# AdaLN transformer layer on one core: both score layouts as two 64-row tiles on TensorE, causal mask by matmuls, row maxima by whole-bank reductions

## The chip, the cores and the metric

The kernel runs on one core of a Trainium2 chip. The metric is the device time of one execution in microseconds (us); the median of three runs of the kernel before is 1957.38 us (1954.21 to 1957.84). TensorE (PE) multiplies, VectorE (DVE), ScalarE (ACT) and GpSimd (POOL) do the rest, SyncE (SP) issues all DMA transfers. PE writes to PSUM (eight banks of 128 partitions x 512 fp32), from which DVE and ACT read.

## The reference, cut to what matters

A layer over x of shape (32, 512, 256), with 16 heads of 16 dimensions:

```python
h = _layernorm(x) * (1 + ca) + sa
q, k, v = split(h @ w_qkv.T + b_qkv)                     # 16 heads of 16
scores = einsum('bhqd,bhkd->bhqk', q, k) / np.sqrt(hd)
scores = scores + where(k_pos <= q_pos, -(q_pos - k_pos), -1e30)   # ALiBi and causal mask
out = einsum('bhqk,bhkd->bhqd', softmax(scores), v)
x = x + ga * (out @ w_out.T + b_out)
h = _layernorm(x) * (1 + cb) + sb
x = x + gb * ffn(h)                                      # gate of 8 experts, top-p count, two experts used
```

The modulation vectors (sa, ca, ga, sb, cb, gb) come from a small product before the layer.

## The kernel before, in words

**Stages.** Each of the 32 batch elements passes through stages of a software pipeline: layer norm and transposition, q/k/v, row maxima, scores and exponentials, weighting of v, output product, second norm, gate, experts. One iteration of the main loop (`iterations`, `one`) has 16 slots, one head of scores in each. The tables `SIDE`, `SP_AT`, `DVE_AT`, `POOL_AT` and `ACT_AT` say which other step ("side step") of which batch element stands in which slot; `PE_ORDER`, `ACT_ORDER` and `DVE_ORDER` are the order within a slot. Every engine executes its own list in order, and semaphores tie the lists together. No planner moves anything.

**Two layouts of the scores.** The exponentials need the scores with keys on partitions ("scores", `0 1 2` in the order strings, banks 0 to 2 of PSUM, L575). Their row maximum is needed first, and is taken from a second computation with queries on partitions ("row scores", `a b c`, banks 3 and 4 in turn, L589), which runs eight heads ahead. Only the ten causal 128x128 blocks of a head's sixteen are computed: 1280 moving columns in each layout. Both contract over one stack of rows: 96 rows hold q and k split into high and low fp16 parts for a pair of heads (the rows of the other head are zeros in `kz`), then the ALiBi row and mask rows up to 112, then the negated maxima up to 114. So each matmul uses all 128 rows of the array, for a head of 16 dimensions.

**Maxima.** DVE reads the pieces a (512 columns), b (384 and 128) and c (256) with `tensor_tensor_reduce`, which adds the mask of the diagonal block (`mask_qk`) and reduces to one column of `mxt` (L853). Each of the four instructions of a head is followed by an instruction that fetches the accumulator. A group of four heads is transposed by PE (side step `mt`, L538), copied by ACT to `negm` and put by DMA into the stack (`load_aug`). PE may write piece k only when DVE has read piece k-2 (`mx_read`).

**Exponentials and weighting.** ACT takes exp of banks 0 to 2 (L647). POOL zeroes the upper triangles of the diagonal blocks by `affine_select` (L1018, semaphore `masked`). PE multiplies with v (`weigh`, L603 and L609), fp32, four heads side by side in 32 output columns each; `w` stands in every slot with one key tile kt, and is a burst of 4 x 128 columns, with a second of 4 x 384, 256 or 128 where kt is 0, 1 or 2.

**Side steps.** qk, v, out and moe are groups of fp16 matmuls of 3072 columns (L497); they use banks 6 and 7 in turn, and each waits for the reader of the step before it in its bank. DVE reads the result of a side step one slot later (`S`, `U`).

## Time and profile before

| | us |
|---|---|
| median of 3 runs | 1957.38 |
| profiled execution, span from first to last instruction | 1953.2 |
| PE busy | 1724.6 (88%) |
| PE weight loads busy | 995.6 (51%) |
| DVE busy | 1552.6 (79%) |
| ACT busy | 1214.8 (62%) |
| POOL busy | 998.9 (51%) |

The page of the profile gives no time outside the span; the lowest run is 1954.21 us, 1.0 us more than the span. Busy time is the union of the instructions' durations. A matmul's duration contains the way of its results through the array, which the next matmul overlaps, so the pitch (start to start) of neighbouring rows tells more of PE than its busy time. The granted TensorE clock, in forty slices of the span, is 8 and 7 tenths in the first two, 9 tenths or more in the next 36, and 8 and 6 tenths in the last two.

### The profile page before, as it was taken

To read this page: it belongs to the slowest core of one execution; us is meant where nothing else is said; L and a number is where in the kernel's file an instruction comes from. 1 tells how busy PE (TensorE), PEld (TensorE's weight loads), DVE (VectorE), ACT (ScalarE), POOL (GpSimd) and SP (SyncE) were. 2 spreads that over 40 slices of the span, in tenths; PEclk is the share of its full clock that TensorE was granted. 3 is DMA by queue.
4 is the path that set the end of the run, shared out by engine and by line. 5 is a ranking of instruction groups with operands and counts; after the bars stand their busy time and mean duration, and the time that the engine had idled before them with its cause. 6 is when DMAs were issued, how large, how long until landed. Compare 5 with 4: busy or idle time off the path is not lost.

```text
span 1953.2 us, 62334 instructions
## 1 busy us (share of the span) xinstructions
PE 1724.6 (88%) x17744; PEld 995.6 (51%) x17744; DVE 1552.6 (79%) x5632; ACT 1214.8 (62%) x2466; POOL 998.9 (51%) x1225
## 2 busy tenths in 40 slices
...
GB/s 131 77 133 116 125 119 128 141 128 124 125 104 125 140 136 126 120 125 120 128 141 128 123 125 104 126 141 136 125 120 125 121 129 139 131 123 115 120 88 45
DMA packets 206753, 238.21 MB, mean 122 GB/s; under 512 B 27626, under 2 KB 153138, under 8 KB 206674
## 3 DMA queue, kind: packets, MB, share of 16 engines
...
q8 instruction: 23, 0.38, 0.1%
...
## 4 chain that ended last, share of the span: by engine, by line
PE 49%; DVE 24%; issue 18%; ACT 4%; DMA 2%; DVEq 2%; POOL 1%; SPq 1%; ACTq 0%; POOLq 0%
PE ps L497 18%; PE ps L589 12%; DVE ps L853 9%; PE ps L575 8%; PE ps L609 4%; PE ps L603 4%; DVE mxt L853 4%; DVE ol L868 2%; DVEq L257 1%; ACT hf_a L658 1%; ACT hh_a L660 1%; DVE qk_st L793 1%; DVE st_c L759 1%; ACT prob L647 1%; PE ps L515 1%
## 5 line engine op out<-in xcount | busy, mean ns | idle before, releaser
L853 DVE CUSTOM_DVE_ANT_0 ps<-ps,mask_qk 128x512 f32<-128x512 f32 (+3 forms) x2048 | 971.1, 510 | 296.3 <-PE ps L589 285.3
L647 ACT ACTIVATE prob<-ps 128x512 f32<-128x512 f32 (+1 forms) x1536 | 743.5, 530 | 363.2 <-PE ps L575 362.3
L589 PE MATMUL ps<-kz,qs 112*128 112x512 f16 (+3 forms) x2048 | 542.4, 307 | 138.2 <-DVE mxt L853 129.5
L1018 POOL TENSOR_SCALAR_AFFINE_SELECT prob<-prob 128x512 f32<-128x512 f32 x512 | 353.4, 696 | 364.2 <-ACT prob L647 364.2
L575 PE MATMUL ps<-qs,kz 114*128 114x128 f16 (+2 forms) x3584 | 453.3, 243 | 3.7 <-DMA qs<-negm 3.1
L589 PEld LDWEIGHTS ps<-kz,qs 112*128 112x128 f16 x2048 | 187.1, 97 | 492.8 <-DVE mxt L853 308.6
L853 DVE DVE_READ_ACCUMULATOR2_ANT mxt<- 128x1 f32 x2048 | 288.6, 141 | 0.0
L575 PEld LDWEIGHTS ps<-qs,kz 114*128 114x128 f16 x3584 | 259.7, 98 | 50.5 <-ACT prob L647 3.8
L609 PE MATMUL ps<-prob,va 128*32 128x384 f32 (+2 forms) x3072 | 237.0, 380 | 0.0
L603 PE MATMUL ps<-prob,va 128*32 128x128 f32 x4096 | 218.3, 285 | 2.0 <-issue 0.9
L679 ACT ACTIVATE qk_st<-ps,bqk 128x512 f16<-128x512 f32 x128 | 88.0, 688 | 97.7 <-PE ps L497 95.7
L992 POOL TENSOR_TENSOR xg<-xc,ga_bc 128x1024 f32<-128x1024 f32 x32 | 75.6, 2361 | 101.6 <-DMA ga_bc<-rows_d 90.5
L986 POOL TENSOR_TENSOR om<-oc,rz 128x1024 f32<-128x1024 f32 x32 | 75.5, 2359 | 95.3 <-DMA rz<-rz_d 95.3
L603 PEld LDWEIGHTS ps<-prob,va 128*32 128x32 f32 x4096 | 81.1, 108 | 84.6 <-issue 81.7
L965 POOL TENSOR_TENSOR rs_c<-ve_c,neg_half 128x4 f32<-128x4 f32 x32 | 32.7, 1022 | 166.4 <-DVE nm_c L774 166.4
L793 DVE SCALAR_TENSOR_TENSOR qk_st<-ps,bqk,qk_st 128x512 f16<-128x512 f32 x128 | 95.6, 747 | 7.1 <-ACT qk_st L679 7.1
L497 PE MATMUL ps<-moe_hi,hh_c 128*128 128x512 f16 x256 | 99.5, 389 | 1.0 <-DVE gsub L826 1.0
L1008 POOL TENSOR_TENSOR zg<-zs,gb_bc 128x512 f32<-128x512 f32 x64 | 81.4, 1271 | 36.1 <-DVE zs L806 35.1
L695 ACT ACTIVATE z<-ps,scl 128x256 f32<-128x256 f32 x128 | 60.5, 473 | 62.9 <-PE ps L497 58.8
L497 PE MATMUL ps<-moe_lo,hh_c 128*128 128x512 f16 x256 | 99.2, 387 | 0.0
L497 PE MATMUL ps<-moe_hi,hl_c 128*128 128x512 f16 x256 | 99.1, 387 | 0.0
L497 PE MATMUL ps<-hh_a,wqkv_hi 128*128 128x512 f16 x256 | 97.9, 382 | 0.4 <-DVE qk_st L793 0.4
...
## 6 DMA issues: line engine op xcount, KB each, us to landing
qk_d<-qk_st SPq DMA_DIRECT2D x128, 256.0 KB, 2.0
ou_d<-ou SPq DMA_DIRECT2D x128, 256.0 KB, 2.0
qs<-qk_d SPq DMA_DIRECT2D x128, 192.0 KB, 2.6
kz<-qk_d SPq DMA_DIRECT2D x256, 96.0 KB, 2.6
...
qk_d<-qk_st SPq DMA_DIRECT2D x128, 128.0 KB, 1.9
...
```

Of the source, the lines that this page charges most:

```text
L497: x_ = mm(dst, a, b, start=(n == 0), stop=(n == len(pairs) - 1))
L575: x_ = mm(ps[:, ST + n, col:col + w * P], kz[0:STACK, h, kt * P:(kt + 1) * P], qs[0:STACK, h // 2, qt * P:(qt + w) * P], start=True, stop= ...
L589: x_ = mm(ps[:, bank, col:col + w], qs[0:CONST, h // 2, qt * P:(qt + 1) * P], kz[0:CONST, h, 0:w], start=True, stop=True)
L603: x_ = mm(ps[32 * j:32 * j + 32, PVB, kt * P:(kt + 1) * P], va[:, kt, h, :], prob[:, h % 8, kt * P:(kt + 1) * P], start=(kt == 0), stop=(k ...
L609: x_ = mm(ps[32 * j:32 * j + 32, PVB, (kt + 1) * P:S], va[:, kt, h, :], prob[:, h % 8, PCOL[kt]:PCOL[kt] + w], start=False, stop=False)
L647: nc.scalar.activation(prob[:, h % 8, at:at + w], ps[:, ST + n, 0:w], ACT.Exp, scale=1.0 / FS).then_inc(s["exp_done"], 1)
L679: nc.scalar.activation(qk_st[:, k, 0, :], src, ACT.Identity, bias=bqk[:, 2 * k + n // 2:2 * k + n // 2 + 1]).then_inc(s["qk_hi"], 1)
L793: v.scalar_tensor_tensor(qk_st[:, kk, 1, :], src, bqk[:, 2 * kk + n // 2:2 * kk + n // 2 + 1], qk_st[:, kk, 0, :], ALU.add, ALU.subtract). ...
L853: x_ = v.tensor_tensor_reduce(ps[:, bank, col:col + w], ps[:, bank, col:col + w], mask_qk[:, S - w:S], 1.0, -3e38, ALU.add, ALU.max, mxt[: ...
L992: q.tensor_tensor(xg[:], xc[:], ga_bc[:, 1:2, :].broadcast_to([P, QT, D]), ALU.add).then_inc(s["xg_ready"], 1)
L1008: q.tensor_tensor(zg[:, t, :], zs[:, t, :], gb_bc[:].rearrange("p (o d) -> p o d", o=1).broadcast_to([P, 2, D]), ALU.mult).then_inc(s["zg_ ...
L1018: q.affine_select(out=d, in_=d, compare_op=ALU.is_ge, fill=0.0, base=0, pattern=[[0, 4], [1, P]], channel_multiplier=-1).then_inc(s["maske ...
```

## The change: what it does

- **Stack.** A head now has its own 64 rows (`HALF`): even heads in partitions 0 to 63, odd heads in 64 to 127: 48 rows of q and k parts, the ALiBi row (49 in all for the row scores) and the maxima row (50 for the scores). `kz` is stored per pair of heads, no zeros are needed, and the mask rows are gone.
- **PE.** `both` issues a matmul of the scores of head t and one of the row scores of head `pos ^ 1` alternately. The two are always in opposite halves of the array's rows and in different banks. The waits for `exp_done` and `mx_read` stand together ahead of the piece.
- **Mask.** In piece 0 of each layout two matmuls (64 rows of a bf16 table of 0 and -1e30 against a repeated identity, 256 columns each) are put into the bank first, and the products of the four diagonal blocks are added. `mask` on POOL and the semaphore `masked` go.
- **Maxima.** Pieces are 4, 4 and 2 blocks. One `tensor_reduce` per piece writes one maximum per block into `mxp`; once per four heads a further `tensor_reduce` (`r`, `rows_max`) gives `mxt`, with absent blocks preset to -3e38. `mt` is one transpose instead of four and ACT copies 16x128 instead of 4x512.
- **Order.** Even slots: `01su2`, odd: `0su12w`; `w` stands only in odd slots with two key tiles (0 and 3, or 1 and 2). Two `v` steps, the `spread` steps and some banks of `SIDE` move.
- **DMA.** A stack load is four transfers of 48 partitions instead of three, `load_aug` is two transfers as before, with 256-byte pieces.

```diff
-PE_ORDER = "01asub2wc"
-ACT_ORDER = "o01su2"
-DVE_ORDER = "SUaboc"
+PE_ORDER = ("01su2", "0su12w")
+ACT_ORDER = ("o01su2", "o0su12")
+DVE_ORDER = "rSUaboc"
 SIDE = {
...
-    5: [("mt", 2, 0, 1)],
-    6: [("gate", 0, -2, 0)],
-    7: [("qk", 2, 1, 1), ("v", 0, 1, 0)],
+    5: [("mt", 2, 0, 1), ("v", 0, 1, 0)],
+    6: [("gate", 0, -2, 1)],
+    7: [("qk", 2, 1, 0)],
...
-    13: [("mt", 0, 1, 0)],
+    13: [("mt", 0, 1, 1), ("v", 1, 1, 0)],
     14: [("out", 0, -1, 1)],
-    15: [("v", 1, 1, 1), ("out", 1, -1, 0)],
+    15: [("out", 1, -1, 0)],
...
+        BLOCKS = [4, 4, 2]
+        MX_AT = [(0, 5), (11, 1), (7, 1)]
+        MOVES = [6, 2, 2]
+        ROWS_AT = [[(0, 0, 1, 0), (1, 1, 1, 1), (2, 2, 1, 2), (3, 3, 1, 3)], [(3, 0, 3, 1), (2, 1, 1, 0)],
+                   [(1, 0, 1, 0), (2, 0, 1, 1)]]
...
+            def score(b, h, n, m):
+                rows = slice(HALF * (h % 2), HALF * (h % 2) + ST_ROWS)
+                half = slice(HALF * (h % 2), HALF * (h % 2) + HALF)
+                bank = ps[:, ST + n, :]
+                if n == 0 and m < 2:
+                    x_ = mm(bank.rearrange("p (t k) -> p t k", t=QT)[:, :, HALF * m:HALF * m + HALF], mask_key(2 + m)[half],
+                            EYE[half].rearrange("p (t k) -> p t k", t=QT), start=(m == 0), stop=False)
+                else:
+                    kt, qt, w = CHUNK[n][m - 2 if n == 0 else m]
+                    col = sum(c[2] for c in CHUNK[n][:m - 2 if n == 0 else m]) * P
+                    x_ = mm(bank[:, col:col + w * P], kz[rows, h // 2, kt * P:(kt + 1) * P],
+                            qs[rows, h // 2, qt * P:(qt + w) * P], start=(n > 0), stop=(n > 0 or m == 5))
...
+            def both(i, t, n):
+                bm, pos = max_at(i, t)
+                hm = pos ^ 1
+                if live(i):
...
+                    wait(pe, "exp_done", i * 48 + 3 * t + n - 2, "passed_pe")
+                if live(bm):
...
+                    wait(pe, "mx_read", bm * 48 + 3 * pos + n - 1, "passed_pe")
+                for m in range(MOVES[n]):
+                    if live(i) and not (n == 2 and m == 1):
+                        score(i, t, n, m)
+                    if live(bm):
+                        row_score(bm, pos, hm, n, m)
...
+            def maxima(b, pos, n):
+                g, h = pos // 4, pos ^ 1
+                at = (h % 2) * 2 + h % 4 // 2
+                wait(dve, "mx_ready", b * 48 + 3 * pos + n + 1, "passed_dve")
+                bank = ps[:, MX + (3 * pos + n) % 2, 0:BLOCKS[n] * P]
+                first, apart = MX_AT[n]
+                v.tensor_reduce(mxp[:, g % 2, at, first:first + apart * (BLOCKS[n] - 1) + 1:apart],
+                                bank.rearrange("p (m k) -> p m k", k=P), AX.X, ALU.max).then_inc(s["mx_read"], 1)
```

On PE, before, the end of one slot of the loop and the start of the next read as follows (L575 scores, L589 row scores, L603 and L609 weighting with v):

```order
L589 MATMUL ps<-kz,qs 128x384 [waits mx_read]
L589 MATMUL ps<-kz,qs 128x128
L575 MATMUL ps<-qs,kz 128x256 [waits exp_done]
L603 MATMUL ps<-prob,va 32x128 x4
L609 MATMUL ps<-prob,va 32x256 x4
L257 REGISTER_ALU
L589 MATMUL ps<-kz,qs 128x256 [waits mx_read]
L575 MATMUL ps<-qs,kz 128x128 [waits exp_done]
L575 MATMUL ps<-qs,kz 128x128 x3
```

Now the end of an odd slot and the start of the even one after it (L586 and L602 mask matmuls, L591 scores, L606 row scores, L637 and L643 weighting):

```order
L259 REGISTER_ALU [waits exp_done]
L591 MATMUL ps<-qs,kz 128x256 [waits mx_read]
L606 MATMUL ps<-kz,qs 128x128 x2
L637 MATMUL ps<-prob,va 32x128 [waits ou_ready,va_ready,exp_done]
L637 MATMUL ps<-prob,va 32x128 x3
L643 MATMUL ps<-prob,va 32x384 x4
L637 MATMUL ps<-prob,va 32x128 x4
L259 REGISTER_ALU [waits exp_done]
L586 MATMUL ps<-mk 128x4x64 [waits mx_read]
L602 MATMUL ps<-mk 128x4x64
L586 MATMUL ps<-mk 128x4x64
L602 MATMUL ps<-mk 128x4x64
```

The two layouts alternate row by row now, the weighting follows both, and a piece of scores waits for DVE too.

On DVE, before, around the step o_lo (L868) of slot 11 (L853 maxima, L806 the side step moe):

```order
L853 ISA ps,mxt<-ps,mask_qk 128x512 [waits mx_ready]
L853 ISA mxt 128x1
L257 REGISTER_ALU
L853 ISA ps,mxt<-ps,mask_qk 128x384 [waits mx_ready]
L853 ISA mxt 128x1
L853 ISA ps,mxt<-ps,mask_qk 128x128
L853 ISA mxt 128x1
L257 REGISTER_ALU [waits om_ready]
L868 SCALAR_TENSOR_TENSOR ol<-om,bv,oh 128x512 [waits out_ready,oh_ready]
L868 SCALAR_TENSOR_TENSOR ol<-om,bv,oh 128x512
```

Now the maxima of two slots, with the group's further reduction between them (L882 maxima, L888 rows_max, L825 the side step qk):

```order
L882 TENSOR_REDUCE mxp<-ps 128x4 [waits mx_ready]
L259 REGISTER_ALU
L882 TENSOR_REDUCE mxp<-ps 128x2 [waits mx_ready]
L888 TENSOR_REDUCE mxt<-mxp 128x16 [waits mx_read,mt_ready]
L259 REGISTER_ALU
L825 SCALAR_TENSOR_TENSOR qk_st<-ps,bqk,qk_st 128x512 [waits qk_hi]
```

Eight instructions per head became three, and one more per four heads.

## Rows read from the trace of the kernel before

**Rows 1.** The page: busy time by engine, and shares of the chain of waits.
```profile
PE 1724.6 (88%) x17744; PEld 995.6 (51%) x17744; DVE 1552.6 (79%) x5632; ACT 1214.8 (62%) x2466; POOL 998.9 (51%) x1225
PE 49%; DVE 24%; issue 18%; ACT 4%; DMA 2%; DVEq 2%; POOL 1%; SPq 1%; ACTq 0%; POOLq 0%
```
**Rows 2.** Windows: length, busy PE, PEld, DVE, ACT, POOL, then clock, DMA share, GB/s.
```profile
1000.00:1057.70 57.70, 52.52 (x553) 30.36 (x553) 47.75 (x176) 37.86 (x77) 30.88 (x38) 1.00 0.38 126
```
**Rows 3.** Timeline, PE, the gate: start us, duration us, engine, line, operation.
```profile
1000.95 0.17 PE L497 MATMUL ps<-gw_hi,hh_c 128*128 128x8 f16 x1
...
1001.53 0.17 PE L497 MATMUL ps<-gw_hi,hl_c 128*128 128x8 f16 x1
...
1578.23 0.17 PE L497 MATMUL ps<-gw_hi,hh_c 128*128 128x8 f16 x1
```
**Rows 4.** Timeline, PE, one slot and its borders.
```profile
1010.40 0.43 PE L603 MATMUL ps<-prob,va 128*32 128x128 f32 x8
1010.65 0.83 PE L609 MATMUL ps<-prob,va 128*32 128x384 f32 x8
1011.41 0.28 PE L589 MATMUL ps<-kz,qs 112*128 112x256 f16 x1
1011.53 0.61 PE L575 MATMUL ps<-qs,kz 114*128 114x128 f16 x6
1011.97 0.38 PE L589 MATMUL ps<-kz,qs 112*128 112x512 f16 x1
1012.19 0.60 PE L538 MATMUL ps<-ident,mxt 128*4 128x128 f32 x4
1012.77 0.39 PE L497 MATMUL ps<-hh_a,wqkv_hi 128*128 128x512 f16 x1
...
1014.07 0.38 PE L589 MATMUL ps<-kz,qs 112*128 112x384 f16 x2
...
1014.50 0.43 PE L603 MATMUL ps<-prob,va 128*32 128x128 f32 x8
1014.74 0.61 PE L609 MATMUL ps<-prob,va 128*32 128x256 f32 x8
1015.29 0.28 PE L589 MATMUL ps<-kz,qs 112*128 112x256 f16 x1
```
**Rows 5.** Timeline, DVE: the gate chain's ends, one head's maxima, ot, o_lo.
```profile
1004.17 0.18 DVE L824 TENSOR_REDUCE gmax<-ps 128x4 f32<-128x32 f32 x1
...
1006.88 0.70 DVE L853 CUSTOM_DVE_ANT_0 ps<-ps,mask_qk 128x512 f32<-128x512 f32 x1
1007.49 0.14 DVE L853 DVE_READ_ACCUMULATOR2_ANT mxt<- 128x1 f32 x1
...
1008.64 0.75 DVE L793 SCALAR_TENSOR_TENSOR qk_st<-ps,bqk,qk_st 128x512 f16<-128x512 f32 x1
...
1021.76 2.89 DVE L868 SCALAR_TENSOR_TENSOR ol<-om,bv,oh 128x512 f16<-128x512 f32 x2
```
**Rows 6.** Timeline, ACT, the slot with the side steps ta.
```profile
1038.48 1.08 ACT L647 ACTIVATE prob<-ps 128x512 f32<-128x512 f32 x2
1039.66 0.78 ACT L658 ACTIVATE hf_a<-ps,mod_a 128x512 f32<-128x512 f32 x1
...
1042.32 1.37 ACT L647 ACTIVATE prob<-ps 128x256 f32<-128x256 f32 x3
```
**Rows 7.** Waits: engine, line, releaser: us in total, times, longest.
```profile
DVE ps L853 <- PE ps L589: 285.3, 416, 3.9
PE ps L589 <- DVE mxt L853: 129.5, 200, 4.1
```
**Rows 8.** One line's instructions: min/median/max ns, first and last start.
```profile
L1018 POOL TENSOR_SCALAR_AFFINE_SELECT prob<-prob x512: 624/635/1104, 75.0 to 1891.4; 128x512 f32<-128x512 f32 x171
L868 DVE SCALAR_TENSOR_TENSOR ol<-om,bv,oh x64: 739/1114/1865, 158.1 to 1918.1; 128x512 f16<-128x512 f32 x64
```
**Rows 9.** The page: the costliest groups, the weight loads of the scores.
```profile
L575 PEld LDWEIGHTS ps<-qs,kz 114*128 114x128 f16 x3584 | 259.7, 98 | 50.5 <-ACT prob L647 3.8
```

More of the change, by code:

```diff
@@ L535, in side_step @@
                 elif name == "mt":
-                    wait(pe, "mx_read", b * 48 + 12 * (n + 1))
-                    for t in range(QT):
-                        x_ = nc.tensor.transpose(dst[0:4, t * P:(t + 1) * P], mxt[:, n, t, :], ident[:])
-                    x_.then_inc(s["mt_ready"], 1)
+                    wait(pe, "mxt_ready", b * 4 + n + 1)
+                    nc.tensor.transpose(dst[0:16, 0:P], mxt[:, n, :], ident[:]).then_inc(s["mt_ready"], 1)
                 elif name == "out":
@@ L566, in side_step @@
                     products(dst, pairs).then_inc(s["moe_ready"], 1)
-            def scores(b, h, n):
-                if h % 4 == 0 and n == 0:
-                    wait(pe, "aug_loaded", (b * 4 + h // 4 + 1) * 32)
-                wait(pe, "exp_done", b * 48 + 3 * h + n - 2)
-                col = 0
-                for kt, qt, w in CHUNK[n]:
-                    x_ = mm(ps[:, ST + n, col:col + w * P], kz[0:STACK, h, kt * P:(kt + 1) * P],
-                            qs[0:STACK, h // 2, qt * P:(qt + w) * P], start=True, stop=True)
-                    col += w * P
-                x_.then_inc(s["st_ready"], 1)
@@ new lines, in row_score @@
+            def row_score(b, pos, h, n, m):
+                rows = slice(HALF * (h % 2), HALF * (h % 2) + MX_ROWS)
+                half = slice(HALF * (h % 2), HALF * (h % 2) + HALF)
+                bank = ps[:, MX + (3 * pos + n) % 2, :]
+                if n == 0 and m < 2:
+                    x_ = mm(bank.rearrange("p (t k) -> p t k", t=QT)[:, :, HALF * m:HALF * m + HALF], mask_key(m)[half],
+                            EYE[half].rearrange("p (t k) -> p t k", t=QT), start=(m == 0), stop=False)
+                else:
+                    qt, kt, w, col = ROWS_AT[n][m - 2 if n == 0 else m]
+                    x_ = mm(bank[:, col * P:(col + w) * P], qs[rows, h // 2, qt * P:(qt + 1) * P],
+                            kz[rows, h // 2, kt * P:(kt + w) * P], start=(n > 0), stop=(n > 0 or m == 5))
+                if m == MOVES[n] - 1:
+                    x_.then_inc(s["mx_ready"], 1)
@@ L618, in one @@
                         experts()
-                    bm, hm = max_at(i, t)
                     bp = i if t >= 4 else i - 1
-                    for what in PE_ORDER:
-                        if what in "012" and live(i):
-                            scores(i, t, int(what))
-                        if what in "abc" and live(bm):
-                            row_scores(bm, hm, "abc".index(what))
+                    for what in PE_ORDER[t % 2]:
+                        if what in "012":
+                            both(i, t, int(what))
                         if what in "su":
@@ L688, in side_step @@
                     wait(act, "aug_loaded", (b * 4 + n) * 32)
-                    nc.scalar.activation(negm[:], ps[0:4, MISC + bank, :], ACT.Copy,
+                    nc.scalar.activation(negm[:], ps[0:16, MISC + bank, 0:P], ACT.Copy,
                                          scale=-1.0 / FS).then_inc(s["nm_ready"], 1)
@@ L725, in one @@
                         act.wait_ge(s["ld_w"], W_LOADS * 16)
-                    for what in ACT_ORDER:
+                    for what in ACT_ORDER[t % 2]:
                         if what in "012" and live(i):
```

162 lines of the change are left out of this document (74 added, 88 removed).

## Prediction

> **What bounds the kernel now.** I read the busy times and the chain of waits first. PE is busy 88% of the span and holds 49% of the chain, DVE 79% and 24%, and 18% of the chain is issue, that is the gaps of hand-overs [rows 1]. So PE and DVE bound it by turns. The waits agree: DVE waits 285.3 us for row scores, PE 129.5 us for the maxima [rows 7], each for the other.
>
> Then the period. The gate's first matmul stands at 1000.95 and ten iterations later at 1578.23 [rows 3]: 57.7 us each. In one such period PE is busy 52.52 us, DVE 47.75, ACT 37.86, POOL 30.88, at the full clock of 2.4 GHz [rows 2]. The diagonal masks run from 75.0 to 1891.4 us, 16 per iteration [rows 8]; I take 31 full periods (the last is thinner), and the 165 us of start and end as unchanged.
>
> Last, one slot on PE where nothing waits [rows 4]. From 1011.41 to 1015.29 it takes 3.88 us: mt 0.58 (1012.19 to 1012.77), qk 1.30 (to 1014.07), weighting 0.79 (1014.50 to 1015.29), the rest 1.21. The eleven score matmuls stream 2560 columns; the six at 1011.53 stream 1024 in 0.44 us, 2.33 a ns, so all of them take 1.10. The wide part of the weighting takes 0.76 with 384 columns (from 1010.65) and 0.55 with 256 (from 1014.74): 0.21 per 128, so 384 columns stream in 0.64 and 0.12 are left for the change from 32-column tiles back to the whole array. Two such changes of shape make 0.24 a slot.
>
> **The cost per pair of slots, before.** The orders alternate after the change, so I add up pairs (slots 0 and 1, 2 and 3, ...). PE: score work and shape changes 2.7 a pair; qk, v, moe, out 1.3 each; ta or t2 0.9 (two times mt's 0.44); gate 0.6 [rows 3]; mt 0.58; weighting of key tiles 0 to 3: 0.85, 0.64, 0.43, 0.21. That gives 5.7, 6.0, 5.7, 6.6, 7.4, 6.0, 6.1, 7.3: 50.7 us, against 52.52 busy, which holds the matmuls' tails. DVE: maxima 1.76 a slot (1006.88 to 1008.64); qk 0.66 and other 512-column steps 0.61 (1006.88 to 1007.49), the moe half 0.4 (half as wide), gates 2.7 (1004.17 to 1006.88), o_lo 2.8, reciprocal, statistics and their ends 0.7 to 0.9 each [rows 5]: 7.5, 4.2, 5.4, 7.1, 4.6, 7.4, 6.4, 4.1: 46.6. ACT: exponentials 1.3 a slot, ta or t2 2.66, a bank's copy 0.5 [rows 6]: 6.2 in the pairs with ta and t2, less elsewhere. The larger of the three in each pair: 7.5, 6.0, 6.2, 7.1, 7.4, 7.4, 6.4, 7.3, in all 55.2. The period is 57.7, so 2.5 us are hand-overs which this sum doesn't see. I keep them.
>
> **The change part by part.**
> Scores on PE. Per slot 1280 columns in either layout, plus 2 x 256 for each layout's mask: 1792 in each half of the array. Side by side they take 1792/2.33 = 0.77 us instead of 1.10; one after the other 1.54. The trace shows no row tiles. The nearest row is the weighting: eight matmuls of 384 columns in four column tiles take 0.64 and the shape change [rows 4]. In turn, at 2.33 columns a ns, eight would take 1.32. So tiles of the array do run at once, and I take 0.78. It saves 0.32 x 16 = 5.1 us a period; at the other end it costs 7.0. The mask matmuls write their 256 columns as four pieces of 64; if that halved their rate, 0.22 a slot would come back, 3.5 us a period; the rows show no such output, and I take 0.
>
> The Trainium skill, page "TensorE: Matmul & The Clock Gate", Part 3, says that four row tiles measured 3.07x, which is in line with the value taken; no run here shows it yet.
>
> Shape changes. `w` in every second slot drops some, but scores and full-array side steps now have different shapes: two in an even slot (01|su|2), four in an odd one (0|su|12|w|). 48 a period instead of 32 and the mt steps' own. A row split may need no such gap, or the same 0.12: 0 to 48 x 0.12 = 5.8 against 4.0 before. I take 0.12: +1.8 us.
>
> The Trainium skill, "TensorEngine Tiling (Array Packing)", Tiling Modes, Key Properties, says that a change of mode drains the engine while a change of tile does not. The gap of 0.12 agrees for column tiles [rows 4]; were it free between the whole array and row tiles, 32 of the 48 changes would go, 3.8 us a period on PE.
>
> mt: 3 of 4 transposes go, 0.33 x 4 = 1.3 us. PE per pair after: 3.35 (scores 1.56, six changes 0.72, weighting 1.07) and the side steps: 4.5, 6.0, 5.8, 5.3, 6.2, 6.0, 6.2, 6.0, in all 46.0.
>
> Maxima on DVE. Two pieces of 512 and one of 256 stay reads of PSUM at one element a cycle: 1280 elements before and after. `tensor_reduce` of 512 is not in the trace. Below: 0.55 (512 at the slope between 128x32 at 0.18 and the 512 of L853). Above: 0.75 as L793 [rows 5]. I take the pitch of 0.61 of the instruction it replaces, 0.35 for 256: 1.57 a slot, 0.19 less; what goes is the fixed part of two pieces, the accumulator reads being hidden already (the one at 1007.49 starts with the next piece). `rows_max` adds 0.2 per four slots, +0.8. Bounds: 1.4 to 1.9 a slot, -5.8 to +2.2 us a period; taken -2.2. DVE per pair after: 7.3, 3.8, 5.2, 6.7, 4.4, 7.0, 6.3, 3.8: 44.5.
>
> POOL loses 512 masks of 0.64 us [rows 8], on no bound now. What it may give is o_lo, whose halves take 739 to 1865 ns with POOL busy beside them: 0 to 1.4 us a period; I take nothing, since zg and res of `finish` still stand there. `mask` also stood ahead of `weigh`; PE hardly waited at it, so 0.
>
> ACT: negm of 128 columns instead of 512, 4 x 0.3 = 1.2 us, partly exposed in the two ACT pairs, but one `v` copy joins the t2 pair: 5.9 and 6.4.
>
> The joint wait. Ahead of each piece PE now waits for exp and for DVE together, and what stands behind is the scores for ACT too. Where DVE is in gates or o_lo (2.7, 2.8 us), PE stops after two more pieces, as before. Bound: 0 (it would have stopped there anyway) to 0.2 a slot, 3 us; I take 0. One more DMA per stack load lies eight heads ahead of its use: 0; without that cover it would cost an issue, some 0.5 us.
>
> **Sum.** Larger of three per pair: 7.3, 6.0, 6.4, 6.7, 6.2, 7.0, 6.3, 6.0 = 51.9; with the 2.5 us of hand-overs 54.4. Five of the eight pairs are DVE's or ACT's now, which is why 4.7 us off PE give only 3.3 a period. 3.3 x 31 = 102 us off the span of 1953.2: 1851, and with the 4.2 us by which the median stands above the span, 1855. Own range 1810 to 1905.
>
> **The rivals.**
> 1. *The tiles don't overlap* (slower). If the two halves run in turn, score work is 1.54 a slot: PE per pair +1.5: 6.0, 7.5, 7.3, 6.8, 7.7, 7.5, 7.7, 7.5. With DVE's 7.3 in the first pair 59.3 + 2.5 = 61.8 us, +4.1 x 31: 2085. It decides from 1.1 us a slot upward. For it: each layout now writes a whole bank's 128 partitions, twice the results at once, which column tiles never did. Against it: the overlap in rows 4, and that this split leaves weights and moving rows in separate partitions. 11%.
> 2. *Weight loads bound the score work.* 19 loads instead of 11 per slot, most of them under 128-column matmuls. If each took its recorded 98 ns [rows 9] in turn, a slot's scores would take 1.86 us, PE per pair +2.2: with DVE's 7.3 in the first pair 63.8 + 2.5 = 66.3, +8.6 x 31: 2225. Against it: the gate's 24 matmuls with 128x128 weights stand 25 ns apart (1000.95 to 1001.53) [rows 3], and the six at 1011.53 take no more than their columns [rows 4], so the recorded 98 ns overlap. 3%.
>
> The Trainium skill, "TensorE: Matmul & The Clock Gate", Back-to-back issue gap, gives about 81 ns for a matmul of 128 columns with its load; by that, 19 of them would take an estimated 1.54 us, as in rival 1. The gate rows don't bear it out.
>
> 3. *Single slots bind, not pairs.* The work is uneven now: an even slot has 1.0 and its side step on PE, an odd one 2.3 and its side steps. With two banks for maxima and three for scores there is little to run ahead. The larger engine slot by slot sums to 56.4 after and 58.7 before (measured: 57.7), a gain of 2.3 x 31 = 71: 1886. With the joint wait at its 3 us a period it is slower by 0.7 x 31 = 22: 1979. Middle: 1925. For it: the issue share of 18% [rows 1], which says how much the engines hand to and fro. Against: an odd slot puts its two DVE pieces ahead of `w`, whose 1.07 covers DVE. 20%.
> 4. *The order hides the DVE stretches.* If `su` covers the maxima throughout, groups of four slots decide: 11.1 (DVE), 11.9 (DVE), 12.2, 12.2 = 47.4, with hand-overs 49.9, with o_lo shorter 49.1: 1690 to 1715. For it: the way back to PE is shorter by the accumulator read of 0.14. Against: five of eight pairs are not PE's. 12%.
>
> **Numbers.** Forecast 54%, rival 3 20%, rival 4 12%, rival 1 11%, rival 2 3%. Likeliest 1855. Range 1710 to 1960: it leaves out half of rival 4 and rivals 1 and 2, 20%, and of rival 3 only its last part. About 0.2%, 4 us, is what can be told from no change. Rival 3 gives 16% to faster, 2% to no change and 2% to slower; so faster 82%, same 2%, slower 16%.
>
> **What would show it.** Right: row scores and scores of a pair start within a few ns of each other, a slot's score rows span 0.78 us of pitch, `tensor_reduce` of 512 has a pitch of 0.61, the gate repeats every 54.4 us, DVE waits less for PE than 285 us, POOL near 650 us busy. Each change of shape around `su` shows 0.12. Wrong: pairs in turn (1.54), a mask matmul longer than its 256 columns (its output lies in four pieces of 64), PE idle behind `mx_read` by over 3 us a period more than now (rival 3), or a period under 51 (rival 4).

## The result, and the profile after

The changed kernel takes 2065.76 us (median of 4 runs, 2060.84 to 2069.36) against 1957.61 us before: 1.055 times as long, 95% interval 1.0536 to 1.0572. It is slower by 108 us where 1855 us had been forecast. The profiled execution took 2060.84 us, its span is 2059.1.

The page after, busy times and chain of waits, answers to [rows 1]:

```profile
PE 1646.7 (80%) x21456; PEld 963.5 (47%) x21456; DVE 1430.0 (69%) x3200; ACT 1187.9 (58%) x2466; POOL 647.9 (31%) x711
PE 40%; issue 16%; DVE 14%; DMA 11%; POOL 7%; ACT 6%; SPq 4%; DVEq 1%; ACTq 1%; POOLq 1%
```

No engine is busier than before, yet the span is longer. PE and DVE together held 73% of the chain and hold 54% now; DMA, POOL and SP's queue rose from 4% to 22%. So a larger part of the chain now runs through short transfers and what waits for them, where [rows 1] showed 4%.

One window of an iteration's length after, the gate's first matmul of two successive iterations, and the clock around one stretch (columns as in [rows 2, 3]):

```profile
1000.00:1061.20 61.20, 50.18 (x672) 29.22 (x668) 44.15 (x99) 36.93 (x78) 20.37 (x23) 0.94 0.36 119
...
1032.00:1033.00 1.00, 0.27 (x1) 0.09 (x1) 0.86 (x3) 1.00 (x2) 0.02 (x1) 1.00 0.34 73
1033.00:1034.00 1.00, 0.40 (x4) 0.14 (x4) 1.00 (x3) 1.00 (x4) 0.00 (x0) 1.00 0.15 41
1034.00:1035.00 1.00, 0.00 (x0) 0.00 (x0) 1.00 (x3) 0.65 (x3) 0.00 (x0) 0.75 0.00 0
1035.00:1036.00 1.00, 0.83 (x15) 0.63 (x19) 1.00 (x4) 0.38 (x1) 0.00 (x0) 0.50 0.01 2
1036.00:1037.00 1.00, 1.00 (x12) 0.33 (x8) 0.81 (x7) 0.00 (x0) 0.00 (x0) 0.50 0.01 2
```
```profile
992.55 0.18 PE L511 MATMUL ps<-gw_hi,hh_c 128*128 128x8 f16 x1
...
1053.78 0.18 PE L511 MATMUL ps<-gw_hi,hh_c 128*128 128x8 f16 x1
```

An iteration takes 61.2 us (mean of 20: 61.25), 57.7 before and 54.4 in the forecast. The granted clock is 0.94 where it was 1.00: after 0.27, 0.40 and 0.00 us of work in three successive microseconds PE falls to 1.2 GHz and stays there for 6.8 us. From 200 to 1850 us this happens 28 times, 170.7 us in all; in the same part of the kernel before it happens not once (there are such stretches only at its start and end). The Trainium skill, "TensorE: Matmul & The Clock Gate", Part 1, section "A second HAM failure mode: psum-queue depth-cycling", describes a kernel whose short idle spells between groups of matmuls made the clock swing between its two levels; the rows above agree.

What such a stretch costs can be read in the changed kernel itself, because its length varies. Two successive iterations, the first with 6.8 us at 1.2 GHz and the second with 3.4:

```profile
262.10:323.50 61.40, 50.07 (x673) 29.24 (x669) 44.18 (x99) 36.96 (x78) 20.07 (x22) 0.94 0.37 119
323.50:383.09 59.59, 48.65 (x673) 28.68 (x669) 44.18 (x99) 36.96 (x78) 20.06 (x22) 0.97 0.38 122
```

The same instructions take 1.8 us less. PE's busy time alone differs by 1.4 us; the rest is a shorter wait ahead of slot 12.

The timeline of PE after, scores (L586, L591) and row scores (L602, L606), answers to [rows 4]:

```profile
1005.64 0.40 PE L637 MATMUL ps<-prob,va 128*32 128x128 f32 x8
1005.98 0.28 PE L586 MATMUL ps<-mk 64*128 64x256 bf16 x1
1005.98 0.28 PE L602 MATMUL ps<-mk 64*128 64x256 bf16 x1
1006.10 0.27 PE L586 MATMUL ps<-mk 64*128 64x256 bf16 x1
...
1006.21 0.22 PE L591 MATMUL ps<-qs,kz 50*128 50x128 f16 x1
...
1006.43 0.32 PE L591 MATMUL ps<-qs,kz 50*128 50x384 f16 x1
1006.43 0.32 PE L606 MATMUL ps<-kz,qs 49*128 49x384 f16 x1
1006.60 0.22 PE L591 MATMUL ps<-qs,kz 50*128 50x128 f16 x1
1006.60 0.22 PE L606 MATMUL ps<-kz,qs 49*128 49x128 f16 x1
1006.75 0.39 PE L511 MATMUL ps<-moe_hi,hh_c 128*128 128x512 f16 x1
...
1008.15 0.28 PE L591 MATMUL ps<-qs,kz 50*128 50x256 f16 x1
...
1008.27 0.27 PE L602 MATMUL ps<-mk 64*128 64x256 bf16 x1
```

The two tiles do run at once: both of a pair start within 0.02 us of each other. A slot's scores take 0.45 (1005.98 to 1006.43), 0.22 (two pitches up to the change of shape) and 0.12 us (1008.15 to 1008.27): 0.79, forecast 0.78. The mask matmul's four pieces of 64 cost nothing (256 columns in 0.11 or 0.12). A change of shape is 0.10: the last pair, 0.05 long, starts at 1006.60 and the experts' matmul at 1006.75.

Four pairs of 128 columns pass in 0.22 us, though a weight load still records 97 ns, as in [rows 9] (the page after):

```profile
L591 PEld LDWEIGHTS ps<-qs,kz 50*128 50x128 f16 x3584 | 271.3, 97 | 389.6 <-issue 337.9
```

DVE after, by form (count, busy us, mean ns, idle before it), and the o_lo step (min/median/max ns), answering to [rows 5, 8]:

```profile
L882 DVE TENSOR_REDUCE mxp<-ps 128x4 f32<-128x512 f32 x1024 | 674.7, 686 | 279.8 <-PE ps L606 279.7
L882 DVE TENSOR_REDUCE mxp<-ps 128x2 f32<-128x256 f32 x512 | 212.7, 415 | 111.5 <-PE ps L606 109.8
```
```profile
L901 DVE SCALAR_TENSOR_TENSOR ol<-om,bv,oh x64: 736/792/1875, 162.6 to 2024.8; 128x512 f16<-128x512 f32 x64
```

Two of them in a row take 1.29 us (0.69 + 0.60), so the pitch of 512 is 0.60, forecast 0.61. The o_lo step fell from a median of 1114 to 792 ns, 0.6 us an iteration: a gain that the forecast had left at zero.

The waits after, answering to [rows 7]; the last two rows are one transfer chain, after and before:

```profile
DVE mxp L882 <- PE ps L606: 389.6, 485, 2.8
PE ps L591 <- DVE mxp L882: 170.7, 137, 2.2
POOL om L1023 <- DMA rz<-rz_d: 197.8, 32, 8.5
POOL om L986 <- DMA rz<-rz_d: 95.3, 31, 3.6
```

Both engines wait longer for each other, PE in fewer waits that are longer on average (1.25 us for 0.65). In an iteration PE stands still for 10.9 us in gaps of over 0.15 us; before, it was 5.1. The largest gaps, as means, stand in slot 1 (0.49 ahead of mt, 1.03 and 1.41 ahead of pieces 1 and 2), slot 5 (1.00 ahead of v), slot 7 (1.60 ahead of piece 2, DVE in the gate chain), slot 12 (1.15 and 1.38 ahead of pieces 0 and 1) and slot 13 (1.11 ahead of v). In the two of slot 12 PE waits for ACT, which comes late to the exponentials because it first rounds POOL's product, and then for DVE, which is in o_lo. Both hang on these rows (SP, POOL, DVE):

```profile
1000.26 0.52 SPq L414 DMA_DIRECT2D rz_d<-zr  x1
1002.28 1.28 SPq L420 DMA_DIRECT2D rz<-rz_d  x2
...
1008.02 2.35 POOL L1023 TENSOR_TENSOR om<-oc,rz 128x1024 f32<-128x1024 f32 x1 [6.02 <-DMA rz<-rz_d]
...
1011.91 2.52 DVE L901 SCALAR_TENSOR_TENSOR ol<-om,bv,oh 128x512 f16<-128x512 f32 x2 [0.42 <-ACT oh L746]
```

The reciprocals are stored and loaded back behind four stack transfers in slot 8. Store, load, POOL's product and ACT's rounding take 11.6 us from issue to o_lo. Before, DVE waited for this input of o_lo twice in the whole kernel, 5.0 us in all; now it waits 32 times, 27.6 us. (In the kernel before PE also stood still 1.5 us behind o_lo, so only a part of the two gaps is new.)

### The profile page after: what moved, and what is told of

Read it like the earlier page. It is cut to its first block, busy times and chain, and to the rows that moved or that the text cites. A ratio compares the mean times of both kernels' runs of the same rounds, so it can differ in the third digit from the quotient of the medians.

```text
span 2059.1 us, 69066 instructions
## 1 busy us (share of the span) xinstructions
PE 1646.7 (80%) x21456; PEld 963.5 (47%) x21456; DVE 1430.0 (69%) x3200; ACT 1187.9 (58%) x2466; POOL 647.9 (31%) x711
## 4 chain that ended last, share of the span: by engine, by line
PE 40%; issue 16%; DVE 14%; DMA 11%; POOL 7%; ACT 6%; SPq 4%; DVEq 1%; ACTq 1%; POOLq 1%
PE ps L511 16%; DMA rz<-rz_d 7%; DVE mxp L882 7%; PE ps L591 7%; PE ps L643 6%; PE ps L637 5%; POOL om L1023 4%; DMA rz_d<-zr 3%; PE ps L586 3%; ACT hh_c L692 2%; POOL x L1037 2%; PE ps L606 2%; DVE ol L901 1%; SPq L385 1%; ACT oh L746 1%
## 5 line engine op out<-in xcount | busy, mean ns | idle before, releaser
L882 DVE TENSOR_REDUCE mxp<-ps 128x4 f32<-128x512 f32 (+1 forms) x1536 | 874.6, 596 | 391.2 <-PE ps L606 389.6
L591 PE MATMUL ps<-qs,kz 50*128 50x128 f16 (+2 forms) x3584 | 494.2, 247 | 183.4 <-DVE mxp L882 170.7
L606 PE MATMUL ps<-kz,qs 49*128 49x128 f16 (+1 forms) x4096 | 502.5, 239 | 2.7 <-DVE mxp L882 2.7
L591 PEld LDWEIGHTS ps<-qs,kz 50*128 50x128 f16 x3584 | 271.3, 97 | 389.6 <-issue 337.9
L606 PEld LDWEIGHTS ps<-kz,qs 49*128 49x128 f16 x4096 | 286.9, 97 | 10.5 <-DVE mxp L882 5.2
L586 PE MATMUL ps<-mk 64*128 64x256 bf16 x1024 | 203.8, 280 | 76.5 <-ACT prob L679 33.8
L643 PE MATMUL ps<-prob,va 128*32 128x384 f32 (+2 forms) x3072 | 257.5, 408 | 0.0
L637 PE MATMUL ps<-prob,va 128*32 128x128 f32 x4096 | 226.9, 296 | 1.0 <-ACT ou L734 0.8
L602 PE MATMUL ps<-mk 64*128 64x256 bf16 x1024 | 207.6, 284 | 5.1 <-DVE mxp L882 2.6
L637 PEld LDWEIGHTS ps<-prob,va 128*32 128x32 f32 x4096 | 113.1, 115 | 116.5 <-issue 72.2
L586 PEld LDWEIGHTS ps<-mk 64*128 64x128 bf16 x1024 | 66.2, 95 | 154.7 <-issue 146.6
L511 PE MATMUL ps<-hh_a,wqkv_hi 128*128 128x512 f16 x256 | 111.4, 435 | 12.3 <-DVE zs L838 11.6
L511 PE MATMUL ps<-wqkv_hi,hh_a 128*128 128x256 f16 x256 | 71.8, 280 | 60.4 <-DVE zs L838 30.0
L734 ACT ACTIVATE ou<-ps 128x512 f32<-128x512 f32 x128 | 76.8, 600 | 63.2 <-PE ps L643 63.1
L511 PE MATMUL ps<-hl_a,wqkv_hi 128*128 128x512 f16 x256 | 108.6, 424 | 0.0
L511 PE MATMUL ps<-hh_a,wqkv_lo 128*128 128x512 f16 x256 | 104.7, 409 | 0.0
L825 DVE SCALAR_TENSOR_TENSOR qk_st<-ps,bqk,qk_st 128x512 f16<-128x512 f32 x128 | 95.3, 744 | 9.4 <-ACT qk_st L711 9.0
## 6 DMA issues: line engine op xcount, KB each, us to landing
qk_d<-qk_st SPq DMA_DIRECT2D x128, 256.0 KB, 2.0
ou_d<-ou SPq DMA_DIRECT2D x128, 256.0 KB, 2.0
oc<-ou_d SPq DMA_DIRECT2D x64, 256.0 KB
```

The costliest lines, as they stand in the source:

```text
L511: x_ = mm(dst, a, b, start=(n == 0), stop=(n == len(pairs) - 1))
L586: x_ = mm(bank.rearrange("p (t k) -> p t k", t=QT)[:, :, HALF * m:HALF * m + HALF], mask_key(2 + m)[half], EYE[half].rearrange("p (t k) -> ...
L591: x_ = mm(bank[:, col:col + w * P], kz[rows, h // 2, kt * P:(kt + 1) * P], qs[rows, h // 2, qt * P:(qt + w) * P], start=(n > 0), stop=(n > ...
L602: x_ = mm(bank.rearrange("p (t k) -> p t k", t=QT)[:, :, HALF * m:HALF * m + HALF], mask_key(m)[half], EYE[half].rearrange("p (t k) -> p t ...
L606: x_ = mm(bank[:, col * P:(col + w) * P], qs[rows, h // 2, qt * P:(qt + 1) * P], kz[rows, h // 2, kt * P:(kt + w) * P], start=(n > 0), sto ...
L637: x_ = mm(ps[32 * j:32 * j + 32, PVB, kt * P:(kt + 1) * P], va[:, kt, h, :], prob[:, h % 8, kt * P:(kt + 1) * P], start=(kt == 0), stop=False)
```

## The experiments

Unless said otherwise, an edit is made on the changed kernel. Times are medians of 4 runs (10 for e16), ratios are to the kernel before with their 95% intervals; before had 1957.2 to 1957.9 us beside them. "Half clock" is the number of stretches at 1.2 GHz from 200 to 1850 us and their total.

**e4: do the tiles overlap?** Row scores take the head of the same half of the array.

```diff
-                hm = pos ^ 1
+                hm = pos
-                g, h = pos // 4, pos ^ 1
+                g, h = pos // 4, pos
```

> The changed kernel with the row scores taken from a head of the same parity as the scores beside them, so that both matmuls of a pair use the same 64 rows of the array and can't run at once. It says what the overlap is worth. If PE's streaming still sets much of the period: 0.7 us a slot more on PE, less what lies in gaps: 5 to 10 us a period, 2220 to 2370. If the overlap is mostly spent in gaps by now (waits and the clock set the period): under 3 us a period, 2066 to 2160; PE would then also be busier and the clock higher than 0.93.

2298.71 us, 1.1715 [1.1674, 1.1757], 233 us above the changed kernel (half clock 20 times, 207.6 us). The same pair now runs in turn (timeline of PE in e4):

```profile
1006.75 0.33 PE L591 MATMUL ps<-qs,kz 50*128 50x384 f16 x1
1006.93 0.33 PE L606 MATMUL ps<-kz,qs 49*128 49x384 f16 x1
```

0.18 apart instead of 0.00. The overlap is real and worth 233 us; it isn't what went wrong. The Trainium skill, "TensorE: Matmul & The Clock Gate", Part 3, measures 3.07 times the speed for four row tiles; here two tiles start together, and no run has four.

**e5: is it the uneven weighting?** `w` with one key tile in every slot again ("01su2w", "0su12w").

> The changed kernel with the weighting in every slot again, one key tile each, behind piece 2. Theory B (single slots bind because the work is uneven: an odd slot has 2.3 us and its side steps on PE): 1 to 2 us a period faster although there are 16 changes of shape more (0.12 each, 1.9 us): 2000 to 2060. Theory A (chains of fixed latency and the clock set the period): no gain, and the added changes of shape show, 2066 to 2110.

2075.89 us, 1.0605 [1.0587, 1.0623]; half clock 66 times, 224.7 us. TensorE's gaps fell from 10.9 to 7.8 us an iteration, and the time did not. Sixteen more changes of shape, at 0.10 us each, and half of 54 us more at half clock, 1.0 us an iteration, make 2.6 us and so account for most of it; that is a sum and not a test. Uneven slots do cause some of the gaps, then, but evening them out did not pay. It was not tried with the clock held, as below, so what unevenness costs at full clock is open.

**e1, e2, e3: the two fixed chains.** e1 stores and loads rz in slot 7; e2 puts the first two `spread` steps, which stood ahead of `residual` on POOL, behind norm_c; e3 does both.

```diff
-    8: [("load_stack", 1, 1), ("store_rz", None, -1), ("load_rz", None, -1), ("store_ou", 0, 0)],
+    7: [("store_rz", None, -1), ("load_rz", None, -1)],
+    8: [("load_stack", 1, 1), ("store_ou", 0, 0)],
```
```diff
+    0: [("spread", 0, 0), ("spread", 1, 0)],
-    14: [("finish", 1, -2), ("spread", 0, 1)],
-    15: [("spread", 1, 1), ("residual", 0, -1), ...
+    14: [("finish", 1, -2)],
+    15: [("residual", 0, -1), ...
```

> The changed kernel with store_rz and load_rz issued in slot 7 instead of behind the stack load of slot 8; nothing else. Theory A (a chain of fixed latency from slot 8 to o_lo in slot 11, some 13.4 us from the store at 1000.26 to the second half of o_lo at 1013.68, now longer than the shortened slots around it): o_lo starts earlier, the PE gaps of 0.95, 1.39 and 1.11 us around 1013 to 1019 shrink by 2 to 3 us a period, so 1970 to 2010 us in all. Theory B (the uneven order of the slots and the joint waits hold the period, the chain only fills gaps that are there anyway): less than 0.5 us a period, 2050 to 2066.

> The changed kernel with the two spread steps taken from ahead of the residual in slots 14 and 15 and put behind norm_c, into slot 0 of the next iteration. Theory A (POOL's order delays x1, for which DVE's statistics wait, behind which the maxima stand; the two PE gaps of 1.00 and 1.41 us at 1033 to 1035 follow, and the drop of the granted clock to half for some 7 us behind them): the waits of DVE for x1 (40 us in all) go, 1 to 1.5 us of gaps a period, and with the clock's drop gone up to 3 us more: 1930 to 2030. Theory B (the gaps at the ta and t2 steps come from ACT's 2.7 us of copies): 2050 to 2066 and the clock stays at 0.93.

> The changed kernel with both earlier edits: store_rz and load_rz in slot 7, spreads in slot 0 behind norm_c. Alone they gave 19 us and 3 us, while the granted clock of PE fell from 0.930 to 0.916 and 0.909. If gains add up: 2043. If the clock eats them (theory C): 2035 to 2050 with a clock near 0.91. If one opened the way for the other: 2000 to 2030.

2046.53 (1.0451 [1.0429, 1.0473]), 2062.93 (1.053 [1.051, 1.0551]) and 2027.76 us (1.0337 [1.03, 1.0374]). e1 gives 19 us, e2 3 us (hardly more than the noise), both together 38. The 2046 us of e1 lie between the ranges of its two theories. In each, half clock became more frequent: 63, 66 and 60 times (228.7, 256.0, 211.6 us) against 28. So the clock took back a part of what the removed waits gave; how much is not separated here.

**e6: does streaming in the gaps help?** Extra matmuls (128x128 weights, 512 columns, into the weighting's bank while it is free) ahead of pieces 1 and 2 of slot 1, 4 and 5.

```diff
+            def filler(i, count):
...
+                wait(pe, "ou_ready", (i - 1) * 4 + 3)
+                for _ in range(count):
+                    mm(ps[:, PVB, :], wqkv_hi[:, 0, 0:P], wqkv_hi[:, 1, 0:S], start=True, stop=True)
```

> The changed kernel with idle work for PE: in slot 1, four whole-array matmuls of 512 columns ahead of piece 1 and five ahead of piece 2, into the bank of the weighting while it is free (nobody reads them; the weighting overwrites them). PE waits there 1.00 and 1.41 us anyway, and behind these gaps the granted clock falls to half for 3.4 to 6.8 us in most periods. Theory C (the idle time makes the clock fall, and the fall costs about 3 us a period): the falls at this place go, some 25 of 28, and the time drops by 40 to 85 us to 1980 to 2025. Theory A/B (the clock's fall lies in other waits and costs nothing): the clock rises but the time stays within 10 us of 2066, or rises by what the fillers displace, up to 2 us a period, 2130.

2033.74 us, 1.0371 [1.0346, 1.0395]: 32 us faster with more work, short of the 40 to 85 expected. Half clock 31 times but 116.0 us instead of 170.7.

**e7, e8: the old table of side steps.** The banks and places of `SIDE` as before, on e2 and on e3.

> The spreads in slot 0 as before, and the table SIDE of the kernel before (v in slots 7 and 15, the banks of slots 6 to 13 as they were). Theory D (v in slots 5 and 13 takes the bank that the step one slot earlier has just filled, so PE waits for its reader: 0.99 and 0.22 us behind ta/t2's copies, 1.11 us behind moe, 0.40 us at qk): these gaps go, up to 2.7 us a period, 1980 to 2020. Rival (slots 7 and 15 with two side steps and the double weighting get too long, 2.3 + 2.6 = 4.9 us on PE, and DVE starves): 2060 to 2100.

> All three: store_rz and load_rz in slot 7, spreads in slot 0, the table SIDE of the kernel before. If the stalls are separate, the gains of each add to what each showed alone: about 19 us below the kernel with the old SIDE. If the period is set by one after the other of them, more.

2140.4 (1.0918 [1.0871, 1.0965]) and 2107.11 us (1.0765 [1.0747, 1.0783]): slower by 77 and 79. e7 lies beyond both its ranges, and e8 is 33 us below e7 where 19 had been expected. Half clock holds 348.2 and 296.9 us here, so part of this is clock. The moved steps were not at fault; they belong to the change.

**e9, e10: orders.** e9 is e3 with VectorE's order `raSUboc` in slot 7, so that the maxima of the first piece stand ahead of the gate chain. e10 is e9 with orders `o01s2u`, `o0s1u2` on ACT and `01su2`, `0s1u2w` on PE.

> The kernel with store_rz and load_rz in slot 7 and the spreads in slot 0 (2028 us, 60.1 us a period), and in slot 7 DVE reads piece a ahead of the gate's chain instead of behind it. PE waits there 1.61 us a period for DVE ahead of piece 2. Theory A (waits at single places set the period, one by one): the 1.6 us go, 31 x 1.6 = 50: 1975 to 1995. Theory B (the time moves to the next wait): less than 0.5 us a period, 2012 to 2028, with a new gap ahead of slot 8.

> As the run before, and in even slots ACT takes the exponential of piece 2 between the two copies of ta or t2, in odd slots the second side step stands between pieces 1 and 2 on PE and ACT. PE waits 1.51 us ahead of piece 2 of slot 1 for that exponential, which stood behind 2.7 us of copies. Theory A: 1 to 1.5 us a period less, 31 to 47 us below the run before. Theory B: within 15 us of it.

2042.68 (1.0412 [1.0359, 1.0465]) and 2014.37 us (1.0281 [1.0248, 1.0314]). e9 removed the 1.6 us gap of slot 7 (0.9 appear in slot 8) and its median is 15 us above e3's, half clock 71 times, 314.0 us, against 60 and 211.6. The runs of the two overlap (2024.58 to 2045.86 and 2016.21 to 2031.77), so it gave nothing of the 50 us expected, but that it costs 15 us is not sure. e10 is 28 us below e9, between the ranges of its two theories.

**e11, e12, e16: the same with the clock held.** Extra matmuls as above in e10 (slots 1, 5 and 12: 2 and 3, 3, 6), in e3 (3 and 6, 4, 7), and in e11 without the VectorE order of slot 7.

> As the run before, with fillers for PE (whole-array matmuls of 512 columns into the free bank of the weighting): 2 and 3 in slot 1, 3 in slot 5, 6 in slot 12. Theory C (the granted clock's falls cost 3 us a period, and come from PE's idle time): no falls in the steady part, 40 to 90 us below the run before. If the waits are gone already, the fillers displace up to 3 us a period: up to 90 above it.

> The kernel with store_rz and load_rz in slot 7 and the spreads in slot 0, with the old orders and with fillers in its four longest gaps: 3 and 6 in slot 1, 4 in slot 5, 7 in slot 12. It has 10 falls of the clock per six periods fewer if theory C holds: the clock at 0.97, and 50 to 90 us below 2028 (1940 to 1980); what is then left against 54.4 us a period is waits alone. If the clock's falls cost nothing: 2020 to 2060.

> The fastest version so far (1938.08 us) with the VectorE order of slot 7 put back (S U ahead of a b c instead of r a S U b o c). At unfilled gaps that order took one wait of 1.6 us away and the time grew by 15 us, with the clock falling from 0.921 to 0.896. If only the clock ate its gain, then at full clock the order is worth its wait: this run is slower than 1938 by 0.3 to 0.9 us x 31 = 10 to 28 us, 1948 to 1966. If the order gives nothing in itself: 1938 within 4 us.

| | without extra matmuls | with | half clock, with |
|---|---|---|---|
| chains moved (e3, e12) | 2027.76 | 1966.96 (1.0053 [1.0036, 1.007]) | 0 |
| and ACT and PE orders (e16) | | 1961.36 (1.0009 [0.9995, 1.0023]) | 0 |
| and VectorE order (e10, e11) | 2014.37 | 1938.08 (0.99 [0.9877, 0.9922]) | 1, 3.4 us |

Apart from the extra matmuls the code of a row is the same: 61 and 76 us. And the VectorE order, which gave nothing in e9, is worth 23 us here (e16, 1954.21 to 1965.41, to e11, 1933.31 to 1941.85). The two tests differ in more than the clock, since e16 and e11 also have the ACT and PE orders. e11 is faster than both kernels, than the kernel before by 1.0%. Windows of 200 to 1850 us in e3, e12 and e11:

```profile
200.00:1850.00 1650.00, 1390.84 (x18286) 806.55 (x18285) 1210.72 (x2714) 1015.16 (x2110) 565.14 (x598) 0.94 0.38 122
```
```profile
200.00:1850.00 1650.00, 1482.09 (x19578) 851.52 (x19577) 1255.07 (x2813) 1056.99 (x2193) 586.89 (x622) 1.00 0.39 126
```
```profile
200.00:1850.00 1650.00, 1479.49 (x19766) 850.49 (x19766) 1270.54 (x2859) 1073.18 (x2233) 595.15 (x633) 1.00 0.40 128
```

In the same 1650 us the other engines get more done (DVE 1210.72, then 1255.07 and 1270.54), at 1.00 instead of 0.94.

**e14, e15: controls.** e14 is e12 with 16 columns instead of 512 in each extra matmul. e15 is the kernel before with 20 of the 512-column ones per iteration.

> As the version with early rz store and load, moved spreads and 20 extra matmuls per iteration (1966.96 us; 2027.76 without the extra matmuls), but each extra matmul has 16 columns instead of 512: the same instructions and the same waits at the same places, hardly any streaming. If the streaming itself keeps the clock: clock about 0.92 and 2025 us (2010 to 2040). If the time came from another effect of the inserted instructions (the wait for ou_ready, the order at which banks come free): it stays near 1967 us.

> Control: the kernel before with 5 of the same extra matmuls ahead of piece 2 in slots 0, 4, 8 and 12, 20 per iteration, 4.3 us of streaming. Its steady part has no stretch at half clock, so if the extra matmuls work by the clock alone they give nothing here and cost what the waits don't hide: 1957 to 2060 us, clock as before. If they help by anything else, it is faster than 1957 us.

e14: 2024.0 us (1991.79 to 2029.42), half clock 56 times, 191.1 us. The four runs lie too far apart for a ratio, but the fastest is 23 us above the slowest of e12 (1968.56), and the median is that of e3: it is the streaming that counts and not the inserted instructions. e15: 2073.05 us, 1.059 [1.0572, 1.0608], 13 us above its range, clock 1.00 as without them: where nothing is at half clock they only cost.

e14 also shows what a stretch costs by where it falls. The gate in e14, each row four iterations after the other:

```profile
1344.08 0.18 PE L515 MATMUL ps<-gw_hi,hh_c 128*128 128x8 f16 x1
...
1585.14 0.18 PE L515 MATMUL ps<-gw_hi,hh_c 128*128 128x8 f16 x1
...
1817.21 0.18 PE L515 MATMUL ps<-gw_hi,hh_c 128*128 128x8 f16 x1
```

The first four take 60.27 us each, with two or three stretches (from about 22, 42 and 55 us behind the gate). The next four take 58.02, with one each, at 22.6; and e12, with none, takes 58.00. So the one or two stretches more, in slots 1 and 5, go with 2.25 us more in the same code. The one in slot 12 costs no more than e12's extra matmuls do. Where its time goes, the row of v in slot 13 shows, in e12 and in e14 with a stretch just ahead of it:

```profile
1382.93 0.28 PE L515 MATMUL ps<-wqkv_hi,hh_a 128*128 128x256 f16 x1 [1.11 <-DVE zs L851]
1611.05 0.34 PE L515 MATMUL ps<-wqkv_hi,hh_a 128*128 128x256 f16 x1
```

At full clock PE stands still for 1.11 us there, waiting for DVE; at half clock it arrives later and doesn't wait.

**e13, e17, e18: the clock's share in the changed kernel itself.** e13 adds 4, 6 (slot 1), 4 (slot 5), 4, 5 (slot 12, pieces 0 and 1) and 4 (slot 13) and changes nothing else. e17 leaves out the four at piece 0 of slot 12 and has 6 at piece 1; e18 is e17 with rz early.

> The changed kernel with nothing but extra matmuls (128x128 weights, 512 columns, result overwritten) where TensorE waits: 4 and 6 ahead of pieces 1 and 2 of slot 1, 4 ahead of v of slot 5, 4 and 5 ahead of pieces 0 and 1 of slot 12, 4 ahead of v of slot 13; 27 per iteration, 5.8 us of streaming. No wait, order or transfer is moved. If the granted clock alone makes the loss: the steady part keeps full clock, granted clock 0.97 to 0.98, and the about 3 us per iteration that half clock costs in the changed kernel come back, 1975 us (1960 to 1995). What is left to 1855 is then waits. If the clock is a by-product of the waits and costs nothing of its own: the extra matmuls can only delay, 2066 us or more.

> The changed kernel with extra matmuls again, without the four ahead of piece 0 of slot 12, which stood 2.43 us in a wait for the copy of ou: 4 and 6 in slot 1, 4 ahead of v in slot 5, 6 ahead of piece 1 of slot 12, 4 ahead of v in slot 13. 24 per iteration, 5.1 us of streaming, nearly all of it in stretches where TensorE stood still. If the clock alone costs what the changed kernel shows at half clock, 3 us per iteration less the waits that half clock hides: full clock in the steady part and 58.5 to 59.5 us per iteration, 1975 to 2005 us. The rest of the 211 us to the forecast is then waits. If it stays at 2066 us with the clock near 0.977, the half clock had lain wholly beside other engines' work, and the waits alone make the loss.

> The same extra matmuls, and rz stored and loaded in slot 7. Without extra matmuls the early rz gave 19 us while the stretches at half clock rose from 28 to 63. If the clock had eaten a part of it: now it gives more, 25 to 40 us below the run with the extra matmuls alone. If 19 us is all it is worth, the distance is 15 to 23 us.

e13: 2079.02 us, 1.0639 [1.0606, 1.0673], a miss, for a reason of its own making (timeline of PE in e13):

```profile
1023.35 1.89 PE L654 MATMUL ps<-wqkv_hi 128*128 128x512 f16 x4 [2.43 <-ACT ou L745]
```

The four wait for ACT's copy of ou and hold the scores behind them; half clock still 22 times. e17: 2015.51 us, 1.029 [1.0273, 1.0308], half clock 11 times, 37.5 us: 50 us of the loss are back, though it misses its range of 1975 to 2005, which took full clock throughout. Two of its iterations without a stretch, by window and gate, and two successive ones, with and without:

```profile
1457.05:1574.95 117.90, 105.76 (x1388) 60.45 (x1385) 88.51 (x198) 73.98 (x155) 40.12 (x44) 1.00 0.38 124
437.40:498.00 60.60, 54.31 (x697) 30.55 (x693) 44.42 (x99) 36.99 (x78) 20.07 (x22) 0.97 0.38 120
498.00:557.35 59.35, 52.86 (x696) 30.25 (x693) 44.26 (x99) 37.00 (x78) 20.07 (x22) 1.00 0.39 123
```
```profile
1457.05 0.18 PE L513 MATMUL ps<-gw_hi,hh_c 128*128 128x8 f16 x1
...
1574.95 0.18 PE L513 MATMUL ps<-gw_hi,hh_c 128*128 128x8 f16 x1
```

58.95 each; the 15 undisturbed ones take 59.1 in the mean. The stretches of e17 stand in slot 12 like the one of e14, and here 3.4 us of it cost 1.25 us (60.60 against 59.35): the wait ahead of v in slot 13, which hid it there, is filled with extra matmuls.

e18: 1982.81 us, 1.0124 [1.0106, 1.0142], half clock never: the early rz is worth 33 us here and 19 without extra matmuls. Some of the 33 is the last half clock of e17. By its undisturbed iterations (58.95 to 59.1 against 58.4) rz itself gives 0.5 to 0.7 us, 17 to 22 us in all, and the rest is clock. So the expected 25 to 40 was met, but not by a larger worth of the wait.

## Why the prediction was wrong

The mechanism stood; two steps around it failed. The forecast counted PE's work by pitches and the trace by busy time, which also holds the matmuls' tails, so the two can be compared only as changes from the kernel before. Per iteration:

| term | forecast | measured | measured from |
|---|---|---|---|
| PE's work at full clock | -4.7 (50.7 to 46.0) | -5.5 (52.5 to 47.0) | busy 50.18 less 3.15 |
| PE standing still | +1.4 (7.0 to 8.4) | +5.8 (5.2 to 11.0) | length less busy time |
| lengthening by half clock | 0 | +3.15 | half of 170.7 us / 27 iterations |
| iteration | -3.3 (57.7 to 54.4) | +3.5 (57.7 to 61.2) | |

The miss is 6.85 x 31 = 212 us; 2065.76 - 1855 = 211. The 3.15 is an upper estimate: it takes PE to be busy all through the stretches.

**One step that failed: the granted clock.** The trace of before stood at 1.00 [rows 2], the sum was made at that clock, and nowhere did it ask whether the changed kernel keeps it. The change packs PE's work into less time and leaves the rest as gaps, and there the clock falls. Up to 3.15 us an iteration are lengthening. Taking the half clock away gives 2.1 to 2.3 back in e17 (61.25 to 59.1, or 58.95), at a price of its extra matmuls that isn't known. So the clock is 65 to 98 us of the 211. That it costs time is shown by e12 against e3, by e14 and e15, and by iterations of one kernel that differ in little but the length of a stretch.

**The other, and the larger: "with the 2.5 us of hand-overs".** What remains at full clock, 3.7 to 4.7 us an iteration, is waiting. The 2.5 us were carried over from a kernel whose slots were longer, and the larger-of-three sum sees busy time, not latency. The edits took 1.9 us of it away, each at full clock: 0.5 from rz (11.6 us from issue to o_lo; e17, e18), 0.4 from the `spread` steps on POOL (58.4 to 58.0 in e12), 0.4 from the ACT and PE orders (57.6, e16), 0.6 from VectorE's order in slot 7 (57.0, e11). Only the first and the last are clean steps; in the two between, the extra matmuls change as well (24, 20 and 14 per iteration). None of the four edits was made on the kernel before, so it isn't shown how much of the 1.9 it would have gained too; for rz its trace says little, since DVE waited 5.0 us in all. The 2.6 still missing to 54.4 were not taken apart: their cause is open. The extra matmuls themselves hold PE for 3.0 us there, and whether any of that is on the path was not tried.

**Point by point.** Scores on PE: 0.79 for 0.78, right. Four pieces of 64: 0, right. Shape changes: 0.10 for 0.12, right. `tensor_reduce`: 0.60 for 0.61 and 0.22 for `rows_max`, right; DVE's busy time is 44.15 against 44.5. POOL 648 us, right; that o_lo would not gain was wrong (0.6 us), and harmless, since o_lo now waits for its input. The fourth transfer of a stack load at 0 was doubtful: it is one more issue, 0.43 us, ahead of the store of rz on SP, and what that costs wasn't measured by itself. Neither was the joint wait, taken at 0 with a bound of 3 us: the 170.7 us that PE waits for DVE's maxima stand at scores (L591) now, where the kernel before waited at row scores alone. It remains an untested rival for the 2.6 us that are open. That POOL's mask cost PE nothing wasn't tested either. ACT is busy 36.9 us where 36.7 was implied (37.86 less 1.2). "DVE waits less for PE than 285" was wrong: 389.6.

**The rivals.** 1 (no overlap): refuted by e4. 2 (weight loads): refuted by the four pairs in 0.22 us, eight loads of 97 ns among them. 4: refuted by the period, 61.2 where it asked for under 51. 3 (single slots bind; its sign was "PE idle behind `mx_read` by over 3 us a period more") was nearest in kind. Its slower end, 1979, was priced at full clock, and at full clock the kernel would take an estimated 1968 to 2001 (2066 less 65 to 98), so it may have been near in size too. But its sign did not come: PE's waits for DVE's maxima rose from 129.5 to 202.5 us (170.7 and three smaller rows), 2.4 a period. Its mechanism as written, unevenness, was neither shown nor excluded by e5.
